# Moving one load of five experts' weights on SyncE's queue, from ahead of the first slot-row loads to behind them

## The reference, cut to what matters

```python
logits = x @ router_weight.T
probs = jax.nn.softmax(logits, axis=-1)
topw, topi = jax.lax.top_k(probs, K)                       # K = 8
...
xe = jnp.zeros((E, C, H), x.dtype).at[flat_e, pos].set(x_rep, mode='drop')   # E = 64, C = 128, H = 256
gu = jnp.einsum('ech,ehf->ecf', xe, gate_up_proj)
g, u = jnp.split(gu, 2, axis=-1)
h = jax.nn.silu(g) * u
ye = jnp.einsum('eci,eih->ech', h, down_proj)
...
y = jnp.sum(y_flat.reshape(-1, K, H) * topw.reshape(-1, K)[..., None], axis=1)
```

## Time and profile before

| what | value |
|---|---|
| median of the runs | 312.08 us (310.94 to 312.69) |
| the profiled execution: its time, and its span from first to last instruction | 315.33 us, 313.5 us |
| mean granted TensorE clock | 0.943 |
| busy: TensorE, VectorE, ScalarE, GpSimd | 276.4, 202.3, 158.8, 158.5 us |
| slot-row loads of SyncE (L444) | 64, 130 KB each, 3.2 us from issue to landing |
| scatter-adds of GpSimd (L601 and L604) | 55 |

### The profile page before, as it was taken

How to read it: one execution, slowest core, us unless ns; L and a number is a source line. 1 busy time by engine, 2 the same in 40 slices (tenths; PEclk the granted TensorE clock), 3 DMA queues, 4 the chain that set the end, 5 groups by cost and what they waited for, 6 DMA issues and landing times.

```text
span 313.5 us, 7225 instructions
## 1 busy us (share of the span) xinstructions
PE 276.4 (88%) x2092; PEld 204.7 (65%) x2092; DVE 202.3 (65%) x619; ACT 158.8 (51%) x462; POOL 158.5 (51%) x156
## 2 busy tenths in 40 slices
PE   7999999898989899779737799999999999999950
PEld 3477577466756567457412388888888887878840
DVE  3396786778767976972341057777677789960286
ACT  4448188436853387354522056666666665860000
POOL 1810000002555454557777737787887778887000
PEclk9588999999999999997985989999999999999995
DMA  6890299999999996922599757999999998665952
GB/s 217 263 313 3 58 334 333 347 382 267 283 306 262 309 285 199 322 96 87 164 344 306 233 155 171 160 160 154 173 154 179 156 154 140 73 77 64 287 174 100
DMA packets 63497, 64.61 MB, mean 206 GB/s; under 512 B 4909, under 2 KB 60402, under 8 KB 63472
## 3 DMA queue, kind: packets, MB, share of 16 engines
q1 hardware_dynamic: 52768, 49.06, 55.8%
q0 software_dynamic: 10704, 15.24, 25.9%
HBM read 35.93 MB, written 28.84 MB: 207 GB/s over the span
## 4 chain that ended last, share of the span: by engine, by line
PE 59%; DVE 14%; DMA 8%; issue 8%; ACT 7%; POOL 2%; SPq 1%; ACTq 0%; POOLq 0%; DVEq 0%
PE bank L1240 12%; PE bank L1254 8%; PE bank L916 5%; PE bank L1231 4%; PE bank L928 3%; PE bank L1022 3%; DMA sum<-stage 2%; DMA arena<-sum 2%; DVE rmax L1382 2%; PE bank L1248 2%; PE bank L992 2%; PE bank L947 2%; PE bank L990 2%; PE bank L944 2%; POOL slot_rows L583 2%
## 5 line engine op out<-in xcount | busy, mean ns | idle before, releaser
L583 POOL DMA_INDIRECT slot_rows<-stage x48 | 48.3, 1006 | 34.1 <-issue 7.4
L1240 PE MATMUL bank<-arena,stage 128*128 (+1 forms) x256 | 54.3, 335 | 0.0
L601 POOL DMA_INDIRECT sum<-kz,stage x26 | 40.1, 1542 | 9.7 <-issue 6.5
L1240 PEld LDWEIGHTS bank<-arena,stage 128*128 128x128 f32 x256 | 41.3, 195 | 1.0 <-ACT stage L817 0.2
L1254 PE MATMUL bank<-arena,stage 96*128 (+1 forms) x128 | 40.3, 397 | 0.0
L817 ACT ACTIVATE stage<-bank 128x256 f32<-128x256 f32 x64 | 24.5, 382 | 25.8 <-PE bank L1231 25.2
L1382 DVE TENSOR_REDUCE rmax<-bank 128x2 f32<-128x512 f32 (+1 forms) x48 | 30.6, 684 | 5.9 <-PE bank L947 5.5
L1574 DVE SCALAR_TENSOR_TENSOR stage<-stage,bank 128x96 f32<-128x96 f32 x64 | 16.3, 254 | 21.2 <-ACT stage L827 20.9
L570 POOL COPY stage<-slot_idx 128x16 uint32<-128x16 uint32 x2 | 0.4, 196 | 58.1 <-DVE slot_idx L1466 58.1
L601 POOL DMA_INDIRECT sum<-stage x17 | 26.2, 1544 | 6.7 <-issue 3.5
L916 PE MATMUL bank<-arena 128*128 128x512 f32 (+1 forms) x64 | 25.9, 529 | 2.9 <-ACT arena L632 2.9
(11 more groups left out here) (199 smaller groups left out, 597.9 us busy)
## 6 DMA issues: line engine op xcount, KB each, us to landing
slot_rows<-zero_row SPq DMA_DIRECT2D x8, 1040.0 KB, 12.2
stage<-slot_rows SPq DMA_DIRECT2D x64, 130.0 KB, 3.2
arena<-in_gate_up SPq DMA_DIRECT2D x8, 768.0 KB, 13.0
sum<-zero_row SPq DMA_DIRECT2D x3, 1152.0 KB, 12.7
arena<-in_down SPq DMA_DIRECT2D x4, 768.0 KB, 14.5
arena<-sum SPq DMA_DIRECT2D x12, 256.0 KB, 6.0
arena<-in_gate_up SPq DMA_DIRECT2D x4, 672.0 KB, 12.5
arena<-in_gate_up SPq DMA_DIRECT2D x2, 864.0 KB, 7.3
```

The source lines that it names most:

```text
L583: pool.indirect_dma_start(slot_rows, bass.IndirectOffsetOnAxis(ap=idx[:, t, k:k + 1], axis=0), src[:, t, :], None, bounds_check=SLOTS - 1, ...
L601: pool.indirect_dma_start(sums[a], where, ye_ring[e % RING], None, bounds_check=ACCROWS - 1, oob_is_err=True, compute_op=ALU.add).then_inc ...
L1240: last = mm(bank[2 + q % 2][:, 0:GU + 1], xeT[:, q % 2, k * CAP:(k + 1) * CAP], expert_w[:, s - 1, k * (GU + 1):(k + 1) * (GU + 1)], start ...
```

## The change

The call that issues experts 43 to 47 (three DMAs of 480 KB, 1.47 MB) stands behind the loop that loads the slot rows of experts 0 to 7, instead of between the wait for the last slots and the wait for `g_scat`. The waits stay where they are. On SyncE the three DMAs are now issued behind expert 7's slot-row load and ahead of expert 8's.

```diff
             sp.wait_ge(v_slot, B * TPB)
-            load_experts(EARLY + AFTER_O, AFTER_QK - AFTER_O, s_lw[3])
             sp.wait_ge(g_scat, 16 * K * (B * TPB - 1))
...
             for j in range(GRP):
                 sp.wait_ge(g_last[j], 16)
                 load_slots(0, j, True)
+            load_experts(EARLY + AFTER_O, AFTER_QK - AFTER_O, s_lw[3])
```

## The result

The changed kernel is slower: its time is 1.0108 times that of the kernel before, 95% interval 1.0059 to 1.0157. That is 3.4 us on 312.9, the median of six runs of the kernel before; the changed kernel's median, also of six, is 317.11 (313.75 to 318.65). The six runs of the kernel before are few and uneven: three are those stated under the kernel before (310.94 to 312.69), the other three took 313.13, 317.84 and 317.38 us. The forecast was 1.0 us and no difference that can be told, so it was wrong. The profiled execution of the changed kernel took 317.54 us with a span of 315.7, against 315.33 and 313.5.

What follows compares the result with a forecast made beforehand. GpSimd's chain of scatter-adds was taken as the bound. Start -2.3, first link +2.2, expert 5 or 6 +0.6, second link and later congestion +0.5 gave +1.0 us: 313.1 us, range 310.2 to 316.0.

Steps and rivals of the forecast that it cites:

- GpSimd's chain of adds: Expert part: the scatter-adds at 1.84 us each set the end; delays or advances there move it one for one.
- the start: Start of the expert part: without the weights beside the last scatters, the first add comes 2.3 us earlier, at 183.5.
- the half clock from 179 to 182 us: TensorE at expert 0: the granted clock of 0.50 behind its 1.96 us idle time goes away.
- the queue: SyncE behind expert 7: expert 8's rows wait behind the weights, which land 8.8 us after issue, and TensorE stalls.
- some 5: TensorE ahead of expert 8: idle about 5 us, with a granted clock of 0.5 behind it.
- First link +2.2: GpSimd, expert 0's add to expert 3's: landing beside the weights takes 7.3 us instead of 5.04.
- 0.6 us late: Expert 5's output, behind expert 8's transposes: ready at 195.25, where GpSimd wants it at 194.63.
- +0.5 for the second link and later congestion: Expert 6's add waiting for expert 3's landing amid the burst of slot-row loads, and later adds: 0.5 us lost.
- the chain of adds stays congested: Slower rival, experts 0 to 12: landings over 5.5 us at several links in a row, +2.7 us, 314.8 us; chance 0.25.
- the forecast's sign for the slow side: GpSimd at expert 9: an add over 2 us later than now shows the forecast wrong on the slow side.
- 6.8 us of room: TensorE's last products: they end at 302.0 and their last part is used at 308.8, so they have room.

Runs made afterwards that it cites:

- e16: Changed kernel plus idle work putting off the last slots and last eight scatters, all weights behind expert 7; 1.041 of the kernel before.
- e9: Kernel before, weights in their old place, plus idle work putting off the last slots and last eight scatters; 1.0233 of the kernel before.
- e17: Changed kernel plus idle work putting off last slots and scatters, weights issued on ScalarE's queue instead of SyncE's; 1.0446 of the kernel before.
- e4: Changed kernel with the weights behind expert 15's slot-row load instead of expert 7's; 1.0121 of the kernel before.

## Why the prediction was wrong

**Right:** that GpSimd's chain of adds, and not TensorE, carries the time to the end. In e16 TensorE stalls 3.47 us and the adds behind expert 3's follow at 1.87 us all the same.

**Right: the start.** Forecast 2.3 us earlier, measured 2.53 at the first add; the half clock from 179 to 182 us is gone. The first of the last eight scatters landed in 2.4 us instead of 4.68, the others in 2.3 to 2.8.

**Right: the queue.** The stall ahead of expert 8 is there, 5.70 us against "some 5". Weights from first issue to last landing: 184.49 to 193.9, 9.4 us against 8.8.

**Wrong: the first link.** "First link +2.2" measured +3.24 (8.28 us against 5.04), and 4.1 in e9 against e16. The 2.0 to 2.65 us that it was taken from are a scatter, and an add that had a start on the loads beside it. In the first profile this error lies under the next one.

**Wrong, and the larger error: expert 5's output.** "0.6 us late" measured 2.86. Its parts: expert 8's transposes at 12.83 from S against 9.67, 3.2 late where 2.7 was forecast. From there to the output 3.62 us (194.64 to 197.72 + 0.54) and not 2.65, since the half clock begins with this very step: the prediction put it on experts 6 and 7 alone. And between the output and the add's start lie 0.8 us (198.26 to 199.04; in the earlier trace rows for expert 5 there was more between them, so it did not show), which the prediction left out. 0.5, 1.0 and 0.8 on top of 0.6 give the 2.86, but for rounding. The forecast's last term, +0.5 for the second link and later congestion, measured 0.36 from expert 5's add to expert 6's.

**Two paths, one add.** The landing of an earlier add and the output of an expert end at the same add, and the later of the two counts. The prediction added them: -2.3, +2.2 and +0.6 make +0.5. With its numbers this did no harm, as the later path gives +0.6. With the measured ones it matters which path is the later. By landing, expert 5's add would be at 3.06 + 8.28 and two intervals of 1.87, 15.1 from S, 0.7 later than before; by TensorE it is at 17.2, 2.9 later, so in the first profile TensorE's path decides and costs 2.1 us that landing alone would not. In e16 the first add is later (5.39), the paths give 17.5 and 17.2, and landing decides. In e17 TensorE's path is free, and what expert 5's add gains (15.60 against 17.47) is lost at expert 6's but for the 0.79. These are sums over single profiles, no experiment. The rival "the chain of adds stays congested", at +2.7, was nearest in size, and the forecast's sign for the slow side came true: expert 9's add is 3.2 us later from S. That the rival's place is several links in a row did not show in the changed kernel, where one wait for a landing is long (a link of 8.28 us; of 10.75 in e4); in e17 it is three links, of 7.11, 8.02 and 8.64.

**Room that was used up.** TensorE carries its stall to the end, as the prediction allowed: the last products run from 285.59 to 309.3 instead of from 278.27 and their last part is used at 311.02. Of the 6.8 us of room some 1.7 are left.

**Not foreseen:** that the whole effect hangs on ScalarE being ready. Where it idles 16.26 us behind its table load, the same change measured 0.995 to 0.9965.

What part of the 1.0108 each path has is not shown: no run with the early ScalarE and without the idle work took one of them away. Which step failed is read from the first profile; that it makes up the 3.4 us of the runs is not shown either, since its pair of executions differs by 1.7 us at the last add and 0.65 at the end, counted from S.

## What to carry to other kernels

A chain of transfers that each wait for the landing of an earlier one has no slack to lend: put a bulk load where that chain has not begun, not where the issuing queue happens to be idle. Moving a load off one engine's queue cures what stands behind it there, not what shares the DMA engines. When two delays end at the same instruction, take the later path, not the sum, and expect from curing it no more than its distance to the other (2.1 us in the first profile, nothing in e16).

## What the runs showed of the hardware

- Scatter-adds beside a bulk load fall to a third: 0.13 to 0.14 MB in 6 us beside 1.47 MB, against 0.39 beside the slot rows alone and 0.39 beside 480 KB. The price is not in proportion to the bytes: 0.6 us for the first link with 0.48 MB, 4.1 with 1.47.
- The granted clock falls to 0.50 behind an idle time of 1.96 us as behind one of 5.70; in the changed kernel it is back at 1.00 from 200 us on.
- In three sets of runs out of five the unaltered kernel took 327 to 328 us instead of 314, and the profiles of all kernels in them have ScalarE idle for 16.05 us or more (mostly 16.1 to 16.4) behind a table load of 1.28 us, with TensorE's transposes done. One chip showed both. What it waits for is open, and so is why the attention part was longer there.
